# Channel attention to ternary network: stores by quarters, weight pieces at other steps, norm parts by tile, context masks later

## The reference, cut to what matters

```python
# fifth: attention between channels
qh = q.reshape(b * h, d // h, m)          # 16 * 8 = 128 units of 8 tokens by 256 channels
qk = einsum('bdm,bdn->bmn', qh, kh) * scale
ret = einsum('bmn,bcn->bcm', softmax(qk), vh)
# sixth
scale = clip(mean(abs(w_g), axis=-1), 1e-8)      # groups of 64 weights, in bf16
w_hat = clip(round(w_g / scale), -1, 1) * scale
gate, up = split(x @ w_hat_gate_up.T)
h = silu(gate) * up
out = rms_norm(h) @ w_hat_proj.T
# seventh: per batch entry of 64 tokens, softmax(q.T @ k * s) applied to v
```

## Time and profile before

| | |
|---|---|
| median of 3 runs | 970.3 us (969.97 to 972.47) |
| the profiled execution | 971.1 us, its span 969.2 us |
| loop of the channel attention, PE | 371.4 to 524 us |
| norm for the ternary network starts | 537.6 us |
| ternary network on PE | 552.9 to 630.7 us |
| busy over the span | PE 68%, DVE 56%, ACT 28%, POOL 27% |
| granted TensorE clock | 0.868 in the mean |

### The profile page before, as it was taken

How to read it: one execution, slowest core, us unless ns; L and a number is a source line. 1 busy time by engine, 2 the same in 40 slices (tenths; PEclk the granted TensorE clock), 3 DMA queues, 4 the chain that set the end, 5 groups by cost and what they waited for, 6 DMA issues and landing times.

```text
span 969.2 us, 10797 instructions
## 1 busy us (share of the span) xinstructions
PE 659.9 (68%) x3659; PEld 420.4 (43%) x3660; DVE 546.8 (56%) x1056; ACT 267.1 (28%) x500; POOL 265.0 (27%) x240
## 2 busy tenths in 40 slices
PE   1101988858676014787785399956449999999992
PEld 1001453643465011344444256733426666666661
DVE  5987567595975988687795823346432222222223
ACT  1610232324230020465466233323112112111110
POOL 5242221165901228005528300010021122121200
PEclk9999989779776555699898699988569999999997
DMA  6200000020050042143322000087600001000004
GB/s 222 50 0 11 1 2 1 1 55 0 1 103 0 0 131 103 63 144 105 97 69 67 1 1 1 0 368 316 270 24 20 28 22 32 22 32 22 28 11 141
DMA packets 33675, 62.11 MB, mean 64 GB/s; under 512 B 5732, under 2 KB 29284, under 8 KB 31268
## 3 DMA queue, kind: packets, MB, share of 16 engines
q1 hardware_dynamic: 21776, 45.88, 14.0%
q10 hardware_dynamic: 9648, 9.64, 3.1%
q0 software_dynamic: 2208, 6.03, 2.0%
HBM read 47.54 MB, written 13.70 MB: 63 GB/s over the span
## 4 chain that ended last, share of the span: by engine, by line
PE 48%; DVE 24%; issue 9%; POOL 7%; DMA 7%; ACT 3%; SPq 1%; POOLq 0%; ACTq 0%; DVEq 0%
PE bank L1624 15%; PE bank L1645 7%; DVE XN L346 5%; PE bank L1264 4%; PE bank L1283 3%; DVE region L1064 3%; DMA channel_maxima<-region 2%; PE bank L529 2%; PE bank L1635 2%; PE bank L925 2%; PE bank L503 2%; PE bank L1759 2%; PE bank L432 1%; PE bank L965 1%; POOL rstd L351 1%
## 5 line engine op out<-in xcount | busy, mean ns | idle before, releaser
L1624 PE MATMUL bank<-region,wide 128*128 x368 | 144.0, 545 | 0.3 <-issue 0.3
L1528 DVE TENSOR_TENSOR wide<-wide,bank 128x448 f32<-128x448 f32 x46 | 28.6, 621 | 125.4 <-ACT wide L1571 125.4
L1064 DVE TENSOR_REDUCE region<-bank 128x2 f32<-128x512 f32 x128 | 81.6, 684 | 25.3 <-PE bank L925 24.1
L1624 PEld LDWEIGHTS bank<-region,wide 128*128 128x128 f32 x368 | 68.9, 192 | 61.7 <-issue 61.7
L925 PE MATMUL bank<-region 128*128 128x256 bf16 x256 | 56.7, 313 | 41.8 <-DMA region<-region 26.5
L988 ACT ACTIVATE region<-bank 128x1024 f32<-128x1024 f32 x64 | 65.6, 1025 | 58.4 <-PE bank L949 53.1
L1645 PE MATMUL bank<-region,XN 128*128 x322 | 73.4, 379 | 1.2 <-DVE wide L1541 1.2
L1432 POOL DMA_INDIRECT choice_results<-wide,to_row x23 | 22.7, 987 | 181.6 <-DVE wide L1541 181.6
L1645 PEld LDWEIGHTS bank<-region,XN 128*128 128x128 f32 x322 | 59.5, 190 | 9.3 <-issue 2.2
L1759 PE MATMUL bank<-ident,XN 128*128 128x128 f32 x96 | 22.5, 424 | 59.0 <-DVE XN L346 47.6
L346 DVE TENSOR_SCALAR XN<-X,meanvar,rstd 128x256 f32<-128x256 f32 x64 | 49.4, 844 | 17.0 <-POOL rstd L351 17.0
(11 more groups left out here) (291 smaller groups left out, 1266.1 us busy)
## 6 DMA issues: line engine op xcount, KB each, us to landing
region<-in_L_ffn_experts_dram SPq DMA_DIRECT2D x8, 2688.0 KB, 19.2
region<-ctx_parts SPq DMA_DIRECT2D x24, 192.0 KB
region<-norm_parts SPq DMA_DIRECT2D x8, 576.0 KB
channel_values<-wide ACTq DMA_DIRECT2D x8, 512.0 KB, 6.3
ctx_parts<-region SPq DMA_DIRECT2D x40, 64.0 KB, 2.1
wide<-in_L_ffn_w_gate_up_dram ACTq DMA_DIRECT2D x4, 512.0 KB, 4.4
wide<-channel_values SPq DMA_DIRECT2D x16, 128.0 KB, 2.6
norm_parts<-region SPq DMA_DIRECT2D x24, 64.0 KB, 2.7
```

What stands on the lines that cost most here:

```text
L1064: e.tensor_reduce(nmax[i % 2][:, at_:at_ + KC], ps(u).rearrange("p (c n) -> p c n", c=KC), AX.X, ALU.max, negate=True).then_inc(s_chan["ma ...
L1624: last = e.matmul(bank[hf][:, 512 * gu:512 * gu + hw], xbT[par][:, P * c:P * c + P], region[:, bass.ds(off + (2 * gu + c) * I8 + hw * hf, ...
```

## The change

The store of a tile's values (512 KB) becomes four stores of a quad each (128 KB), each issued right behind the copy of its quad; the semaphore counts follow. DVE's pieces 2 to 5 stand at steps 14, 24, 36 and 48; ACT's casts at 4, 12, 20 and 28. POOL does pieces 0 and 1 first, then piece i + 2 ahead of the add of tile i. The parts of the norm for the ternary network are made for one tile of 128 columns at a time, the first ahead of the tiles and the next at the head of each tile's step; PE waits for the tile's own parts. POOL makes the context masks behind the power of tile 6 and not ahead of the tiles, after all norm parts are made.

```diff
--- before.py
+++ after.py
@@ -859,13 +859,13 @@
             e.dma_start(QS[i % RING][ROWS:ROWS + 3, :, :].rearrange("j u d -> j (u d)"),
                         n_dram[i].rearrange("(j r) m -> j (r m)", j=3)).then_inc(s_chan[f"maxima_in{i % 2}"], 16)
 
-        def act_values_out(e, i):
-
-            e.wait_ge(s_chan["values_copied"], 4 * (i + 1))
-            e.dma_start(o_dram[i].rearrange("q p d -> p q d"), OALL[i % 2]).then_inc(s_chan[f"values_stored{i % 2}"], 16)
+        def act_values_out(e, i, q):
+
+            e.wait_ge(s_chan["values_copied"], 4 * i + q + 1)
+            e.dma_start(o_dram[i, q], OALL[i % 2][:, q, :]).then_inc(s_chan[f"values_stored{i % 2}"], 16)
 
         def values_in(e, i):
-            e.wait_ge(s_chan[f"values_stored{i % 2}"], 16 * (i // 2 + 1))
+            e.wait_ge(s_chan[f"values_stored{i % 2}"], 64 * (i // 2 + 1))
             if i >= 2:
                 e.wait_ge(x_done, 4 * NT + i - 1)
             v = o_dram[i].rearrange("q (g r) d -> (q g) r d", g=4)
@@ -1005,12 +1005,12 @@
                 q, i = w // 2, w // TP5
                 e.wait_ge(s_chan["values_made"], q + 1)
                 if i >= 2:
-                    e.wait_ge(s_chan[f"values_stored{i % 2}"], 16 * (i // 2))
+                    e.wait_ge(s_chan[f"values_stored{i % 2}"], 64 * (i // 2))
                 e.activation(OALL[i % 2][:, q % 4, :], ps(6, 0, D), ACT.Copy).then_inc(s_chan["values_copied"], 1)
 
             def values_out(w):
-                if w % TP5 == TP5 - 1:
-                    act_values_out(e, w // TP5)
+                if w % 2 == 1:
+                    act_values_out(e, w // TP5, w // 2 % 4)
 
             def weights(w):
                 if w in CASTS:
@@ -1019,7 +1019,7 @@
                     if c + 2 < TW // TCH:
                         act_ternary_load(e, c + 2)
 
-            CASTS = {8: 2, 16: 3, 24: 4, 32: 5}
+            CASTS = {4: 2, 12: 3, 20: 4, 28: 5}
             pair_steps([(weights, 0), (maxima_T, 2), (probs, BEHIND), (values, BEHIND + 2), (values_out, BEHIND + 2)])
 
         def split_q(e, ch, i, rest):
@@ -1031,10 +1031,11 @@
             for i in range(3, NT):
                 e.wait_ge(s_chan["norm_split"], i)
                 split_q(e, ch, i, qrest[1])
+            for c in range(2):
+                pool_ternary_weights(e, ch, c)
             for i in range(NT):
-
-                if i < TW // TCH:
-                    pool_ternary_weights(e, ch, i)
+                if i + 2 < TW // TCH:
+                    pool_ternary_weights(e, ch, i + 2)
                 add_values(e, ch, i)
 
         def add_values(e, ch, i):
@@ -1049,7 +1050,7 @@
             for i in range(3):
                 split_q(e, ch, i, qrest[0])
 
-            EARLY, LATE = {26: 2, 50: 3}, {38: 4, 41: 5}
+            EARLY = {14: 2, 24: 3, 36: 4, 48: 5}
             for c in range(2):
                 vec_ternary_weights(e, ch, c)
 
@@ -1079,11 +1080,7 @@
                 if w in EARLY:
                     vec_ternary_weights(e, ch, EARLY[w])
 
-            def weights_late(w):
-                if w in LATE:
-                    vec_ternary_weights(e, ch, LATE[w])
-
-            pair_steps([(weights_early, 0), (maxima, 0), (invert, BEHIND + 14), (weights_late, BEHIND + 14)])
+            pair_steps([(weights_early, 0), (maxima, 0), (invert, BEHIND + 14)])
 
         def later(w, n):
             return not isinstance(w, int) or w >= n
@@ -1155,12 +1152,16 @@
         def vec_ternary(e, ch):
             vec_norm(e, ch, 5)
 
-            for hf in range(2):
-                e.wait_ge(s_turned, TURN["tern"] + 2 * hf + 2)
-                cols = slice(512 * hf, 512 * hf + 512)
+            def parts(i):
+                e.wait_ge(s_turned, TURN["tern"] + KC * (1 + i // 4))
+                cols = slice(P * i, P * i + P)
                 split3(e, ch, XT6[:, :, cols], x6rest[:, :, cols], [a[:, :, cols] for a in x6]).then_inc(s_tern["norm_split"], 1)
 
+            parts(0)
+
             def hidden(i):
+                if i + 1 < NT:
+                    parts(i + 1)
                 for hf in range(2):
                     e.wait_ge(s_tern["silu_ready"], 2 * i + hf + 1)
                     if i >= 2:
@@ -1197,7 +1198,7 @@
 
         def pool_masks(e, ch):
 
-            e.wait_ge(s_rstd, 6)
+            e.wait_ge(s_tern["norm_split"], NT)
             ch.link(e.memset(C1[0:T, :], 0.0))
             ch.link(e.tensor_copy(C1[T:P, :], C[T:P, :]))
             e.memset(C[T:P, :], 0.0).then_inc(s_batch["ctx_masked"], 1)
@@ -1205,10 +1206,11 @@
 
         def pool_ternary(e, ch):
             pool_norm(e, 5)
-            pool_masks(e, ch)
             for i in range(NT):
                 e.wait_ge(s_tern["mean_square"], i + 1)
                 e.tensor_tensor(sinv[:, i:i + 1], ssq[:, i:i + 1], half_neg[:, 0:1], ALU.pow).then_inc(s_tern["rms_inverted"], 1)
+                if i == NT - 2:
+                    pool_masks(e, ch)
 
         def act_ternary(e, ch, turned):
             for g, (dst, _) in enumerate(t6_blocks()):
@@ -1251,7 +1253,7 @@
             e.wait_ge(s_tern["weights_T_ready"], 6)
 
             def gate_up(i):
-                e.wait_ge(s_tern["norm_split"], 1 + i // 4)
+                e.wait_ge(s_tern["norm_split"], i + 1)
                 for hf in range(2):
                     if i == 0:
                         e.wait_ge(s_turned, TURN["tern"] + 4)
```

## The result

The changed kernel takes 986.2 us (median of 4 runs, 979.1 to 988.6) where the kernel before takes 970.1 beside it (4 runs, 966.7 to 972.5): ratio 1.0156, interval 1.0095 to 1.0217, slower by 0.95 to 2.2%. The profiled execution took 985.2 us, its span 983.4; from 372 to 530 us, the loop, its granted clock was 0.76 in the mean (before 0.87). The mean over the whole span (0.819, before 0.868) says little: over the executions of the kernel before it lies between 0.824 and 0.874, and the low ones are not the slow ones. The prediction was 982.3 us, slower.

The account below looks back on a forecast made before the run. Bound taken: the chain of waits to the ternary stage's end, and DVE and POOL blocking each other. Loop +23.5 and tail -11.55 gave +11.95 us: 982.3 us as median, likeliest case 976 to 988, wider range 965 to 988.

Parts of the forecast that it names:

- Rival 3: Quads clog ACT in the loop and each issue reaches PE: +4 us on the forecast, 986 us; chance 0.07.
- (b): Tile 1, piece at step 14: DVE's split meets POOL's piece and ends with it, +8.5 us; +3.8 without meeting.
- (e): Step 36: DVE's and POOL's pieces meet, PE idles, clock falls; tile ends 8.1 us later, +1.6 without meeting.
- rival 1: DVE and POOL do not meet at steps 15 and 36, pieces fall clean: 961.7 us; chance 0.17.
- (c): Tile 2: clock falls after PE idled 5 us, +2.1 less 0.4 for a maxima wait, +1.7 us.
- (d): Piece at step 24 in place of 26: longer PE idle +0.7 and a clock fall +2.0, together +2.7 us.
- (g): Piece at step 48 in place of 50: one clock fall as before but earlier, +1.5 us.
- Rival 2: DVE and POOL meet but the clock does not fall again, giving back 8 us: 974.3 us; chance 0.16.
- (a): Tile 0's split: POOL's piece 1 runs right behind piece 0, one more cast can wait, +1.0 us.
- (f): Tile 5, steps 40 to 47: 0, since POOL's instruction gates the split behind the maxima wait.
- rival 4: Quads free the loop: waits of 5 us go, pieces hide in what is left, loop -2, 957 us; chance 0.05.
- The tail: After the last copy: last fetch -2.1, late masks -4.8, norm parts -2.85, clock at first ternary matmuls -1.8; sum -11.55 us.

Follow-up runs that it names:

- e6: Changed kernel with POOL's piece 2 held until DVE's split of tile 1 is done and piece 3 until DVE's piece 4 left its signs: 973.8 us, ratio 1.0033.
- e7: Changed kernel with identity matmuls, results unused, filling PE's stops at steps 15, 16, 25, 37, 48, 49 and 56: 978.4 us, ratio 1.0081.
- e4: Kernel before with only the norm parts made tile by tile: 965.1 us, ratio 0.9945.
- e3: Kernel before with only the context masks moved behind the power of tile 6: 966.8 us, ratio 0.9951.
- e11: Kernel before with masks late and norm parts by tile, no quads, pieces as before: 963.3 us, ratio 0.9934.
- e5: Kernel before with only the stores by quads: 972.9 us, ratio 1.0033 (1.0 to 1.0065).
- e2: Kernel before with only the weight pieces moved (DVE's steps, ACT's casts, POOL's order): 991.9 us, ratio 1.0228.
- e8: Changed kernel with pieces back at their old steps, but DVE's last two at steps 64 and 65, ahead of the inversion: 963.9 us, ratio 0.9937.
- e12: Quads, parts, late masks; DVE's pieces at 26, 41, 64, 65, POOL's away from splits; identity matmuls in PE's stops: 952.9 us, ratio 0.9824 against kernel before.

## Why the prediction was right

Direction and range held, and so did the mechanism of the loop: DVE's and POOL's pieces meet, and the clock falls behind PE's stops. 986.2 came against 982.3, inside 965 to 988. That the sum lies so near is part luck, told below. Rival 3 had put 986 for clogged quads, which is the measured time; the traces show another cause. By its own steps:

- **(b) and (e), the pieces that meet**, 16.6 of the 23.5 us: 8.9 and 7.2 measured, 16.1. The release of POOL by DVE's own last operation fixed the distance at step 14, as argued against rival 1. e6 takes the meetings away and gets 8.8 us of the two tiles back; the clean price of (e), +3.4, was put too low at +1.6.
- **(c), (d), (g), the clock falls** at 2.0 us each: e7 shows the price for tiles 3, 4, 6 and 7. For (c) the fall is seen (0.50 from 416.6 to 420.0) and the tile's +1.5 fits, but no run takes it away. Rival 2 is out. What did not hold is the line that I drew between a stop of 3.14 us and one of 3.42: with the same loop the clock stayed up behind the first in the kernel before and e4, and fell in e3 and e11 (3.15 us).
- **(a)** +1.4 where +1.0 stood: a cast and a subtraction waited. L378 took 2.05 us at 386.88. The Trainium skill, SBUF — State Buffer, Who interferes with whom, says that operations with two SBUF inputs contend too; by that rule, the trace agrees. In the split of tile 1 the subtractions took 0.19 all the same, between two POOL operations, and the split ended with the piece either way.
- **(f)** 0: -0.4. The gate behind the maxima wait is confirmed by e5. So rival 4 is out. Rival 3, a clogged ACT, is out with e2: the tiles are the same with and without quads, with the clock falling at the same places; e5's interval alone would still hold its 4 us.
- **The tail**: -6.9, -2.6, -1.9 against -6.9, -2.85, -1.8. Masks and parts each stand alone (e3, e4). The last of the three is luck: I argued that a gap of 0.9 us keeps the clock up, and in e6, e7 and e8 it was 0.93 and the clock low. Only four of the ten traces with parts by tile have this gain.
- **The last fetch** was right in sum (-2.1) and wrong in its owner: the quarter gives 0.4 of it and the missing POOL piece 1.7. The Trainium skill, DMA: Bandwidth & Descriptors, Anatomy of one DMA, with its fixed cost, pointed the right way: 2.92 us for 512 KB and 2.60 for 128 KB. The same section adds a part that grows with the bytes, which the prediction left out: by it, as an estimate, the quarter lands 0.9 us sooner, where the traces show 0.3.

The loop came to +27.0 where the sum was +23.5. **The terms that were too small** are the end of tile 6 and tile 7. (g) was put at +1.5 with "one fall as before", and tile 7 at 0. In the trace the split of tile 6 met POOL (L377 at 512.71, 1.98 us), PE stopped for 2.37 and 0.34 us and the granted clock was 0.58 over 515 to 519; e7 gets 2.5 and 1.5 us back by the clock alone. I had priced falls only for stops of over 3 us, from the earlier trace rows, and had left the splits behind the later pieces without one. But such falls are not the change's alone: tile 7 takes 15.4 to 15.6 us in e3, e4 and e11 too, with no piece moved, and the loop of the trace that I worked from is 2 to 3 us shorter than theirs. Set against their loops the changed one is longer by 24 to 25 us and not by 27, near the sum. In the profiled executions the rest came back by chance, the 2.3 us of clock in the eighth block, where nothing was changed. So the sum is right in its large terms, and its last 3 us are beyond what one trace of a kernel can tell.

**What stays open**: how much of the 0 to 0.65% of e5 is the quads' own, beyond 0.3 us; what decides, from one execution to the next, behind which stop the clock falls; and what remains between e6's 12.3 us by its median and the 9.8 in the loop of its trace. That trace is of the slowest of its ten executions (978.1 us) and pays 1.8 and 2.3 us of clock at the network's start and in the eighth block.

## What to carry to other kernels

Where GpSimd does elementwise work on SBUF, place its instructions by what VectorE does meanwhile. Here the reductions from PSUM lay beside them at no cost (five in 3.06 us), casts and small operations waited (1.98 us for 0.18), and a large piece on each side at once took VectorE twice its time (8.95 us for 4.1). A wait that goes is worth only what the next gate leaves of it (here 0.34 of 2.2 us). Look at the granted clock behind each stop of TensorE, short ones too, and try matmuls with unused results in the stop. And before a difference of 1 or 2 us between two traces is given a cause, look at the same stretch in a third kernel whose code there is unchanged: here tile 3 takes 16.5 or 17.6 us with the same loop.

## What the runs showed of the hardware

- The length of a stop did not decide whether the clock fell. Stops of 2.37 and 0.34 us stood ahead of 0.58 (515 to 519), and 3.14 us ahead of 424.89 in the kernel before left the clock up; with the same loop 3.15 us stood ahead of 0.57 in e3 (424 to 428). At the start of the ternary network gaps of 1.15 and 1.23 us stood ahead of 1.00, of 1.32 ahead of 0.58 and of 0.93 ahead of 0.68 (e6).
- The same 48 matmuls of the eighth block took PE 8.33 us at a granted clock of 0.62 and 10.67 at 0.50, in kernels that don't differ there.
- Identity matmuls of 128 columns in the stops held the clock at 1.00 at four of e7's five places and at the two of e12 shown; at e7's steps 15 and 16 it fell all the same (0.51 over 415 to 421). No tile of e7 is more than 0.4 us longer for them.
- The stores of the turned maxima landed in 3.8 us in the median with quads, 6.1 before, though the bytes are the same; the worst case stayed (6.8 and 7.1).
